# A four-block graph network on one core: two whole-state VectorE operations cut into tiles, and broadcast weight and bias rows read from PSUM

## The chip, the cores and the metric

The kernel runs on one core of one Trainium2 chip. The metric is the device time of one execution in microseconds (us); below 0.2% (about 9 us) a measurement of this kernel cannot tell a difference from no change.

## The reference, cut to what matters

A graph of 3125 nodes with 128 features and 53125 edges goes through four residual blocks. Each gathers a row per edge, scales it and sums it into the node that the edge points to. The second block does so five times (DEPTH = 5), with a layer norm that has a gain and a bias after each.

```python
h = relu(layernorm(x)); x = x + segment_sum(edge_weight * h[src], dst) @ W0.T + b0
h = relu(layernorm(x)); y = h
for i in range(5):
    Wf  = (ssp(rbf @ fw1[i] + fb1[i]) @ fw2[i] + fb2[i]) * C      # one filter row per edge
    agg = segment_sum((y @ lin1_w[i])[src] * Wf, dst) / degree
    y   = y + ssp(agg) @ lin2_w[i] + lin2_b[i]
    y   = (y - mean(y)) * rsqrt(var(y) + 1e-5) * ln_g[i] + ln_b[i]
x = x + y
...  # two more blocks of the same kind: one gated by tanh, one that only counts
```

## The kernel before, in words

Nodes are kept as `x`, `x2`, `y` [128 partitions, TILES = 25 tiles, 128 features], 3200 numbers in a partition; `u` is another name of `x`. The trace leaves numbers out of names, so `x2` is `x` there. Edges are worked in GROUPS = 52 groups of 1024. For each group GpSimd (POOL) issues eight indirect DMAs of 128 rows each (line 598, a "gather" below) into one of RING = 10 slots of `rows`. It may start a slot again once VectorE (DVE) has written the next indices into it (`stage`, line 1138).

The 52 groups are walked eight times: `first_edges` for the first block, `conv_edges` for each of the five layers (four in a device loop, `Fori(0, DEPTH - 1)`, and the last behind it), `gated_edges` and `count_edges`. A walk's gathers read the table that the walk before has written, so POOL starts a walk when the last rows of that table are stored.

In a layer, per group: TensorE (PE) makes hidden units and filters, ScalarE (ACT) and VectorE the softplus (`softplus_rest`, line 1335), VectorE adds the filter bias out of PSUM (`take_filters`, line 1342) and multiplies it by the gathered rows (`messages`, line 1348, which waits for the gathers of its group), and PE sums the messages into `sum_ps`, the first 80 columns of a bank of `pD`. The node work of finished blocks is put between the groups by hand (`conv_due`).

Each engine runs its own instructions in program order. `own(...)` makes VectorE wait for its own instruction before the next. Between two layers VectorE brings the state `y` up to date for the layer that begins (lines 1538 to 1541), before its first `softplus_rest`. Before the first layer it scales `y` and adds the bias (1518, 1519), and reads the node degrees, which PE writes into columns 0 to 24 of the same bank of `pD` (1522). Line 1513 adds the first block's bias row to `x`, and line 1543 the last layer's bias row to `x2`.

Of the kernel before, what the change touches and what calls it, by code (L numbers as in the profile page):

```python
# [21 lines left out]
ALU = mybir.AluOpType  # L22
# [3 lines left out]
P = 128  # L26
N_NODES = 3125
N_EDGES = 53125
D = 128
DEPTH = 5  # L30
# [16 lines left out]
TILES = -(-N_NODES // P)  # L47
# [22 lines left out]
def build(nc, a, out):  # L70
    ctx = ExitStack()
    with ctx:
        def sb(name, shape, dt=F32):
            return ctx.enter_context(nc.sbuf_tensor(name, shape, dt))

        def pb(name):
            return ctx.enter_context(nc.psum_tensor(name, [P, 2 * 512], F32))
# [54 lines left out]
        x = sb("x", [P, TILES, D])  # L132
        x2 = sb("x2", [P, TILES, D])
        u = x
        y = sb("y", [P, TILES, D])
# [6 lines left out]
        w0, w3, b0 = (node_log[:, n * D:(n + 1) * D] for n in range(3))  # L142
# [8 lines left out]
        mv = sb("mv", [P, TILES, 2])  # L151
        neg_mean = sb("neg_mean", [P, TILES])
        var = sb("var", [P, TILES])
        rstd = sb("rstd", [P, TILES])
# [16 lines left out]
        lb2 = sb("lb2", [P, DEPTH, D])  # L171
        ln_g = sb("ln_g", [P, DEPTH, D])
        ln_b = sb("ln_b", [P, DEPTH, D])
# [11 lines left out]
        pA, pB, pC, pD = pb("pA"), pb("pB"), pb("pC"), pb("pD")  # L185
# [2 lines left out]
        sum_ps = pD[:, 0:WIN]  # L188
        node_ps_all = pD[:, 512:1024]
        node_ps = node_ps_all[:, 0:2 * P]  # L190
        deg_sum_ps = pC[:, 0:WIN]

        dst_rows_loaded = sem("dst_rows_loaded")
# [78 lines left out]
        def over_tiles(row, n):  # L272
            return row.unsqueeze(1).broadcast_to([P, n, D])
# [226 lines left out]
        with nc.Block() as block:  # L500
# [553 lines left out]
            def _(dve):  # L1054
                n_pass = dve.value_load(passes_i[0:1, 0:1], min_val=1, max_val=MAX_PASSES)

                def own(ins):
                    ins.then_inc(dve_own, 1)
                    dve.wait_ge(dve_own, 1)
                    dve.sem_inc(dve_own, -1)  # L1060
# [114 lines left out]
                def improve_root(root, arg):  # L1175
                    dve.wait_ge(guess_full, 1)
                    dve.sem_inc(guess_full, -1)
                    tmp = newton[:, 0:root.shape[1]]
                    own(dve.scalar_tensor_tensor(tmp, root, -0.5, root, ALU.mult, ALU.mult))
                    own(dve.tensor_tensor(tmp, tmp, arg, ALU.mult))  # L1180
                    own(dve.scalar_tensor_tensor(root, tmp, 1.5, root, ALU.add, ALU.mult))
# [39 lines left out]
                def first_edges():  # L1221

                    def build(g):
                        match(onehot[:, g % 2, :, :], g).then_inc(onehot_full, 1)

                    with dve.Fori(0, n_pass):
                        build(0)
                        build(1)
                        for g in range(GROUPS + 1):
                            for b in done(g - 1):  # L1230
                                first_state(b)
                                node_deviation(b)
                                first_rows(b)
                            if g < GROUPS:
                                add_sums(g, degrees=True, rows_read=True)
                                if g + 2 < GROUPS:
                                    build(g + 2)
                            for b in done(g):
                                dve.sem_inc(agg_full, 1)
                        next_pass()  # L1240
                    last_sum()
# [170 lines left out]
                def begin_conv(l):  # L1412
                    dve.tensor_copy(fw1_l[:, :], fw1[:, l, :])
                    dve.tensor_copy(nfb1_l[:, :], nfb1[:, bass.ds(l, 1)]).then_inc(filter_ready, 1)
                    own(dve.tensor_copy(fb1_l[:, :], fb1[:, bass.ds(l, 1)]))
                    dve.sem_inc(bias_ready, 1)
                    start_sums()
# [81 lines left out]
                        next_pass()  # L1499
                    last_sum()  # L1500

                def over_nodes(tile):
                    return tile[:, :].unsqueeze(2).broadcast_to([P, TILES, D])


                dve.wait_ge(degs_set, 1)
# [3 lines left out]
                own(dve.tensor_tensor(dst0_g, dst0_g, base0[:, :].unsqueeze(2).broadcast_to([P, GROUPS, CH]), ALU.subtract))  # L1510
                start_windows()
                prepare_weights()
                dve.tensor_tensor(x[:, :, :], x[:, :, :], over_tiles(b0[:, :], TILES), ALU.add)
                first_edges()
                dve.sem_inc(deg_full, 1)
                begin_conv(0)

                own(dve.tensor_tensor(y[:, :, :], y[:, :, :], over_nodes(rstd), ALU.mult))
                own(dve.tensor_tensor(y[:, :, :], y[:, :, :], over_tiles(lb2[:, 0, :], TILES), ALU.add))
                dve.wait_ge(deg_ps, 1)  # L1520
                dve.sem_inc(deg_ps, -1)
                own(dve.tensor_scalar(deg_col[:, :], pD[:, 0:TILES], 1.0, None, ALU.max))
                dve.sem_inc(var_full, 1)
                improve_root(dcol[:, :], deg_col[:, :])

                own(dve.tensor_scalar(deg[:, :], deg[:, :], 1.0, None, ALU.max))
# [8 lines left out]
                with dve.Fori(0, DEPTH - 1) as l:  # L1535
                    conv_edges(l, last=False)
                    begin_conv(l + 1)
                    own(dve.tensor_tensor(y[:, :, :], u[:, :, :], mv[:, :, 0:1].broadcast_to([P, TILES, D]), ALU.subtract))
                    own(dve.tensor_tensor(y[:, :, :], y[:, :, :], over_nodes(rstd), ALU.mult))
                    own(dve.tensor_tensor(y[:, :, :], y[:, :, :], over_tiles(ln_g[:, l, :], TILES), ALU.mult))  # L1540
                    own(dve.tensor_tensor(y[:, :, :], y[:, :, :], over_tiles(lb2[:, l + 1, :], TILES), ALU.add))
                own(dve.memset(score[:, N_NODES:NPAD + WIN], 0.0))
                own(dve.tensor_tensor(x2[:, :, :], x2[:, :, :], over_tiles(ln_b[:, DEPTH - 1, :], TILES), ALU.add))
                conv_edges(DEPTH - 1, last=True)
                dve.sem_inc(dots_full, 1)
                start_sums()
# [26 lines left out]
```

## Time and profile before

| | |
|---|---|
| three runs | 4440.54, 4443.06 (median) and 4443.99 us |
| the profiled execution | 4444.43 us, of which the trace spans 4442.6 us |
| busy share of the span | POOL 73%, PE 56%, DVE 51%, ACT 48% |
| mean granted TensorE clock | 0.64 of full speed |

The 1.83 us that the profiled execution's time has over its span lie outside the trace. Busy shares are means over eight walks and their seams; the rows below look at the seams.

### The profile page before, as it was taken

What the parts mean: (1) busy time and instruction counts of PE and PEld (TensorE: products, weight loads), DVE (VectorE), ACT (ScalarE), POOL (GpSimd) and SP (SyncE); (2) the same over time, 40 slices, a digit from 0 to 9 for tenths busy, and PEclk for the clock granted to TensorE, in tenths of its full rate; (3) what the DMA queues carried; (4) which work ended last, traced back from release to release, by engine and by line L of the source; (5) the groups of instructions that cost most, each with busy time, mean ns of one, the idle gap of its engine ahead of it and who ended that gap; (6) DMA issues with size and microseconds to landing.
All of it is one profiled execution on the core that took longest, in us unless ns stands there. A gap on an engine that the chain in (4) does not pass through costs nothing. (4 is left out here: it accounts for less than half of the span.)

```text
span 4442.6 us, 56169 instructions
## 1 busy us (share of the span) xinstructions
PE 2495.7 (56%) x13164; PEld 2233.2 (50%) x13164; DVE 2255.9 (51%) x7419; ACT 2152.1 (48%) x5584; POOL 3251.0 (73%) x3339
## 2 busy tenths in 40 slices
PE   2554456666566665667656676567763333334334
PEld 2544456565455654656546566466663333333333
DVE  3322256666666666666666666677763333322221
ACT  2444456655566655665555665556653545510000
POOL 5777767777677776777767777677774777767776
PEclk8555567777677776777767777666665555555555
DMA  6333222222222222222222222222221222212221
GB/s 131 99 99 99 78 61 69 68 71 58 62 70 69 70 58 64 67 71 68 58 64 67 71 68 58 62 67 68 68 57 39 58 57 58 57 49 56 55 56 53
DMA packets 193643, 297.41 MB, mean 67 GB/s; under 512 B 81669, under 2 KB 116194, under 8 KB 193302
## 3 DMA queue, kind: packets, MB, share of 16 engines
q0 software_dynamic: 106496, 219.17, 19.2%
q10 hardware_dynamic: 33974, 57.75, 4.6%
q1 hardware_dynamic: 52832, 16.73, 1.6%
q8 instruction: 118, 1.93, 0.2%
q14 instruction: 223, 1.83, 0.1%
HBM read 272.15 MB, written 21.27 MB: 66 GB/s over the span
## 5 line engine op out<-in xcount | busy, mean ns | idle before, releaser
L598 POOL DMA_INDIRECT rows<-table,staged_src x3328 | 3244.4, 975 | 1175.8 <-issue 890.8
L770 PE MATMUL pD<-scatter,msg 128*128 128x80 f32 x4160 | 755.5, 357 | 682.1 <-PEq L768 673.9
L770 PEld LDWEIGHTS pD<-scatter,msg 128*128 128x128 f32 x4160 | 713.1, 266 | 757.7 <-issue 757.6
L691 PE MATMUL pD<-scatter,rows 128*128 128x80 f32 x2496 | 572.0, 423 | 665.2 <-PEq L683 360.5
L762 PE MATMUL pC<-fw,hidden 128*128 (+1 forms) x4160 | 819.5, 375 | 184.6 <-PEq L760 183.7
L691 PEld LDWEIGHTS pD<-scatter,rows 128*128 128x128 f32 x2496 | 544.4, 330 | 690.5 <-issue 690.5
L762 PEld LDWEIGHTS pC<-fw,hidden 128*128 128x128 f32 x4160 | 770.9, 284 | 216.0 <-issue 215.2
L908 ACT ACTIVATE scatter<-onehot,c_e 128x80 f32<-128x80 bf16 x2080 | 549.4, 346 | 669.1 <-ACTq L906 669.0
L1348 DVE TENSOR_TENSOR msg<-msg,rows 128x512 f32<-128x512 f32 x520 | 336.7, 688 | 592.9 <-DVEq L1142 588.1
L1131 DVE TENSOR_SCALAR onehot<-win,dst_rel 128x80 bf16<-128x80 f32 x2912 | 557.1, 285 | 31.4 <-DVEq L1060 31.1
L1138 DVE COPY staged_src<-src_i 128x8 int32<-128x8 int32 x416 | 76.0, 183 | 752.2 <-DVEq L1150 752.2
L942 ACT ACTIVATE hidden<-hidden 128x512 f32<-128x512 f32 x520 | 327.6, 630 | 63.6 <-ACTq L833 3.6
L941 ACT ACTIVATE hidden<-hidden 128x512 f32<-128x512 f32 x520 | 327.5, 630 | 62.9 <-ACTq L833 1.6
L1342 DVE TENSOR_TENSOR msg<-pC,fb 128x512 f32<-128x512 f32 x520 | 333.9, 681 | 8.2 <-DVEq L1341 8.1
L940 ACT ACTIVATE hidden<-pA,fb_l 128x512 f32<-128x512 f32 x260 | 176.2, 678 | 241.9 <-ACTq L950 241.9
L908 ACT ACTIVATE scatter<-onehot,w_e 128x80 f32<-128x80 bf16 x416 | 110.3, 347 | 276.1 <-ACTq L906 276.1
L1335 DVE SCALAR_TENSOR_TENSOR hidden<-pA,nfb_l,hidden 128x512 f32<-128x512 f32 x260 | 192.8, 741 | 59.5 <-DVEq L1334 59.4
L1335 DVE SCALAR_TENSOR_TENSOR hidden<-pB,nfb_l,hidden 128x512 f32<-128x512 f32 x260 | 193.3, 744 | 56.9 <-DVEq L1334 56.0
L1024 ACT ACTIVATE gate<-score,rows 128x80 f32 x416 | 110.6, 348 | 208.1 <-ACTq L1021 200.3
L752 PE MATMUL pA<-basis,fw_l 32*128 32x512 f32 x520 | 168.4, 723 | 36.6 <-PEq L749 36.6
L940 ACT ACTIVATE hidden<-pB,fb_l 128x512 f32<-128x512 f32 x260 | 174.0, 669 | 0.1
L752 PE MATMUL pB<-basis,fw_l 32*128 32x512 f32 x520 | 168.3, 723 | 0.0
(195 smaller groups left out, 1681.3 us busy)
## 6 DMA issues: line engine op xcount, KB each, us to landing
rows<-table,staged_src POOLq DMA_INDIRECT x3328
basis<-basis_d ACTq DMA_DIRECT2D x130, 256.0 KB, 2.8
table<-node_rows SPq DMA_DIRECT2D x66, 128.0 KB
msg<-in_edge_weight_dram ACTq DMA_DIRECT2D x54, 128.0 KB, 3.5
basis_d<-basis ACTq DMA_DIRECT2D x26, 256.0 KB, 3.7
hidden<-in_edge_weight_dram ACTq DMA_DIRECT2D x48, 128.0 KB, 3.3
table<-node_rows SPq DMA_DIRECT2D x11, 132.0 KB
out_dram<-node_rows SPq DMA_DIRECT2D x11, 128.0 KB
```

The lines of the kernel that those rows point to most:

```text
L598: pool.indirect_dma_start(out=rows[:, s, j, 0:width], out_offset=None, in_=tab[:, :], in_offset=bass.IndirectOffsetOnAxis(ap=staged_src[:, ...
L691: mm = pe.matmul(sum_ps, rows[:, g % RING, j, 0:D], scatter[:, g % 2, j, :], start=(j == 0), stop=(j == CH - 1))
L752: pe.matmul(hid_ps[n], fw1_l[at, :], basis[at, t % BASIS_RING, :], start=True, stop=True)\
L762: mm = pe.matmul(filt_ps[h][:, c * D:(c + 1) * D], hidden[:, strip(g, h), c * P:(c + 1) * P], fw2[:, l, :], start=True, stop=True)
L770: mm = pe.matmul(sum_ps, msg_of(g, h)[:, c * D:(c + 1) * D], scatter[:, g % 2, HALF * h + c, :], start=(h == 0 and c == 0), stop=(h == 1 a ...
L908: ins = act.activation(scatter[:, g % 2, j, :], onehot[:, g % 2, j, :], ACT.Copy, scale=weights[:, g * CH + j:g * CH + j + 1])
L940: own(act.activation(dst, arg, ACT.Abs, **bias))
L942: act.activation(dst, dst, ACT.Ln, bias=1.0).then_inc(full, 1)
L1131: ins = dve.tensor_scalar(dst[:, j, :], win[:, :], dst_rel[:, g * CH + j:g * CH + j + 1], None, ALU.is_equal)
L1335: dve.scalar_tensor_tensor(hidden[:, n, :], hid_ps[n], nfb1_l[:, 0:1], hidden[:, n, :], ALU.max, ALU.add).then_inc(ssp_full, 1)
L1342: dve.tensor_tensor(msg_of(g, h).rearrange("p (c d) -> p c d", d=D), filt_ps[h].rearrange("p (c d) -> p c d", d=D), over_tiles(fb2[:, l, : ...
L1348: dve.tensor_tensor(part, part, rows[:, g % RING, h * HALF:(h + 1) * HALF, 0:D], ALU.mult)\
```

## The change

Three things. The operations on the whole state that took a mean or a deviation per node from a broadcast tensor become one instruction per tile (25 of them), in which the mean and the deviation are scalars per partition; in the loop subtraction and multiplication become one instruction. Each broadcast row (gain, bias) is first copied from SBUF into a free part of the bank of `pD` (columns 128 to 511; `in_bank`), and the operation on the whole state reads it there. Before the first layer the bias is added behind the reading of the degrees instead of ahead of it.

```diff
+        spread_ps = pD[:, P:4 * P].rearrange("p (n d) -> p n d", d=D)
...
-                def over_nodes(tile):
-                    return tile[:, :].unsqueeze(2).broadcast_to([P, TILES, D])
+                def in_bank(n, row):
+                    own(dve.tensor_copy(spread_ps[:, n, :], row))
+                    return over_tiles(spread_ps[:, n, :], TILES)
+
+                def centred(state):
+                    for t in range(TILES):
+                        ins = dve.tensor_scalar(y[:, t, :], state[:, t, :], mv[:, t, 0:1], rstd[:, t:t + 1], ALU.subtract, ALU.mult)
+                    own(ins)
...
-                dve.tensor_tensor(x[:, :, :], x[:, :, :], over_tiles(b0[:, :], TILES), ALU.add)
+                dve.tensor_tensor(x[:, :, :], x[:, :, :], in_bank(0, b0[:, :]), ALU.add)
...
-                own(dve.tensor_tensor(y[:, :, :], y[:, :, :], over_nodes(rstd), ALU.mult))
-                own(dve.tensor_tensor(y[:, :, :], y[:, :, :], over_tiles(lb2[:, 0, :], TILES), ALU.add))
+                for t in range(TILES):
+                    ins = dve.tensor_scalar(y[:, t, :], y[:, t, :], rstd[:, t:t + 1], None, ALU.mult)
+                own(ins)
                 dve.wait_ge(deg_ps, 1)
                 dve.sem_inc(deg_ps, -1)
                 own(dve.tensor_scalar(deg_col[:, :], pD[:, 0:TILES], 1.0, None, ALU.max))
                 dve.sem_inc(var_full, 1)
+                own(dve.tensor_tensor(y[:, :, :], y[:, :, :], in_bank(1, lb2[:, 0, :]), ALU.add))
                 improve_root(dcol[:, :], deg_col[:, :])
...
-                    own(dve.tensor_tensor(y[:, :, :], u[:, :, :], mv[:, :, 0:1].broadcast_to([P, TILES, D]), ALU.subtract))
-                    own(dve.tensor_tensor(y[:, :, :], y[:, :, :], over_nodes(rstd), ALU.mult))
-                    own(dve.tensor_tensor(y[:, :, :], y[:, :, :], over_tiles(ln_g[:, l, :], TILES), ALU.mult))
-                    own(dve.tensor_tensor(y[:, :, :], y[:, :, :], over_tiles(lb2[:, l + 1, :], TILES), ALU.add))
+                    gain, bias = in_bank(0, ln_g[:, l, :]), in_bank(1, lb2[:, l + 1, :])
+                    centred(u)
+                    own(dve.tensor_tensor(y[:, :, :], y[:, :, :], gain, ALU.mult))
+                    own(dve.tensor_tensor(y[:, :, :], y[:, :, :], bias, ALU.add))
...
-                own(dve.tensor_tensor(x2[:, :, :], x2[:, :, :], over_tiles(ln_b[:, DEPTH - 1, :], TILES), ALU.add))
+                own(dve.tensor_tensor(x2[:, :, :], x2[:, :, :], in_bank(2, ln_b[:, DEPTH - 1, :]), ALU.add))
```

On VectorE, at the end of the loop body and behind the loop, the kernel before has these rows (line, operation, output and inputs, size, count; ISA and REGISTER_ALU rows set up addresses):

```order
L1538 TENSOR_TENSOR y<-x,mv 128x3200
L1539 TENSOR_TENSOR y<-y,rstd 128x3200
L1540 ISA
L1540 TENSOR_TENSOR y<-y,ln_g 128x3200
L1541 REGISTER_ALU
L1541 TENSOR_TENSOR y<-y,lb 128x3200
L1535 REGISTER_ALU
L1535 COMPARE_AND_BRANCH
L1542 MEMSET score 128x155
L1543 TENSOR_TENSOR x<-x,ln_b 128x3200
```

At the same place on VectorE the changed kernel has:

```order
L1504 ISA
L1504 COPY pD<-ln_g 128x128
L1504 REGISTER_ALU
L1504 COPY pD<-lb 128x128
L1509 TENSOR_SCALAR y<-x,mv,rstd 128x128 x25
L1549 TENSOR_TENSOR y<-y,pD 128x3200
L1550 TENSOR_TENSOR y<-y,pD 128x3200
L1544 REGISTER_ALU
L1544 COMPARE_AND_BRANCH
L1551 MEMSET score 128x155
L1504 COPY pD<-ln_b 128x128
L1552 TENSOR_TENSOR x<-x,pD 128x3200
```

Two of the four long operations have become 25 short ones, and the others, with the one behind the loop, take their row from `pD` after a copy each.

On VectorE ahead of the first layer, from the state's scaling to the first operation on `deg`, the kernel before has:

```order
L1518 TENSOR_TENSOR y<-y,rstd 128x3200
L1519 TENSOR_TENSOR y<-y,lb 128x3200
L1522 TENSOR_SCALAR deg_col<-pD 128x25
L1179 SCALAR_TENSOR_TENSOR newton<-dcol 128x25
L1180 TENSOR_TENSOR newton<-newton,deg_col 128x25
L1181 SCALAR_TENSOR_TENSOR dcol<-newton,dcol 128x25
L1526 TENSOR_SCALAR deg<-deg 128x3280
```

There the changed kernel has:

```order
L1526 TENSOR_SCALAR y<-y,rstd 128x128 x25
L1530 TENSOR_SCALAR deg_col<-pD 128x25
L1504 COPY pD<-lb 128x128
L1532 TENSOR_TENSOR y<-y,pD 128x3200
L1180 SCALAR_TENSOR_TENSOR newton<-dcol 128x25
L1181 TENSOR_TENSOR newton<-newton,deg_col 128x25
L1182 SCALAR_TENSOR_TENSOR dcol<-newton,dcol 128x25
L1535 TENSOR_SCALAR deg<-deg 128x3280
```

The long bias operation has moved from ahead of the degrees to behind them.

## Rows read from the trace of the kernel before

**Rows 1.** The page's first line, and line 598: duration in ns min/median/max.

```profile
span 4442.6 us, 56169 instructions
...
L598 POOL DMA_INDIRECT rows<-table,staged_src x3328: 940/944/4147, 35.1 to 4432.9; - x196
```

**Rows 2.** POOL's waits: us in total, times, longest us.

```profile
POOL rows L598 <- POOLq L596: 285.0, 405, 39.3
```

**Rows 3.** Timeline, second layer's start: start us, us, instruction [idle before <-releaser].

```profile
1131.37 4.01 POOL L598 DMA_INDIRECT rows<-table,staged_src  x1 [17.00 <-POOLq L596]
...
1134.72 3.49 DVE L1539 TENSOR_TENSOR y<-y,rstd 128x3200 f32<-128x3200 f32 x1
...
1135.69 3.34 POOL L598 DMA_INDIRECT rows<-table,staged_src  x1 [0.31 <-issue]
...
1156.84 1.29 DVE L1348 TENSOR_TENSOR msg<-msg,rows 128x512 f32<-128x512 f32 x2 [0.35 <-DVEq L1142]
```

**Rows 4.** Line 598 by stretch: us, POOL busy (gathers), PEclk, DMA share, GB/s.

```profile
80.80:84.20 3.40, 3.33 (x1) 0.50 0.08 22
575.10:583.10 8.00, 7.48 (x2) 0.50 0.03 8
1131.30:1146.60 15.30, 14.19 (x4) 0.50 0.34 99
2790.20:2809.70 19.50, 18.10 (x5) 0.50 0.27 81
606.80:739.50 132.70, 101.15 (x104) 0.72 0.25 67
1243.00:1343.90 100.90, 76.71 (x80) 0.79 0.26 70
```

**Rows 5.** Timeline at 71 us: VectorE reads PSUM while a gather is made.

```profile
71.75 0.81 DVE L1091 TENSOR_TENSOR lb<-lb,pB 128x640 f32<-128x640 f32 x1
71.82 0.94 POOL L598 DMA_INDIRECT rows<-table,staged_src  x1 [0.30 <-issue]
```

**Rows 6.** Timeline: VectorE operations with scalars, and the gather beside each.

```profile
586.78 1.87 DVE L1526 TENSOR_SCALAR deg<-deg 128x3280 f32<-128x3280 f32 x1
587.00 2.46 POOL L598 DMA_INDIRECT rows<-table,staged_src  x1 [0.30 <-issue]
...
2893.72 0.60 DVE L1388 TENSOR_SCALAR x<-x,mv,rstd 128x128 f32<-128x128 f32 x2 [0.15 <-DVEq L1060]
2893.90 0.99 POOL L598 DMA_INDIRECT rows<-table,staged_src  x1 [0.30 <-issue]
...
4101.40 1.65 DVE L1131 TENSOR_SCALAR scatter<-win,dst_rel 128x80 f32<-128x80 f32 x8 [0.24 <-DVEq L1060]
4102.07 0.94 POOL L598 DMA_INDIRECT rows<-table,staged_src  x1 [0.30 <-issue]
```

**Rows 7.** VectorE's groups by line and shape: busy us, mean ns | idle before.

```profile
L1388 DVE TENSOR_SCALAR x<-x,mv,rstd 128x128 f32<-128x128 f32 x25 | 7.6, 344 | 1.8 <-DVEq L1060 1.8
L1096 DVE TENSOR_SCALAR score<-lin,ln_gT 128x128 f32<-128x128 f32 x4 | 0.9, 283 | 0.1
```

**Rows 8.** Timeline, first layer: last gather of groups 0 and 14, and their messages.

```profile
591.02 0.94 POOL L598 DMA_INDIRECT rows<-table,staged_src  x1 [0.30 <-issue]
...
610.07 1.33 DVE L1348 TENSOR_TENSOR msg<-msg,rows 128x512 f32<-128x512 f32 x2 [0.35 <-DVEq L1142]
...
738.49 0.95 POOL L598 DMA_INDIRECT rows<-table,staged_src  x1 [0.30 <-issue]
...
741.77 1.29 DVE L1348 TENSOR_TENSOR msg<-msg,rows 128x512 f32<-128x512 f32 x2 [0.26 <-DVEq L1142]
```

**Rows 9.** VectorE's timeline ahead of the first layer, from the degrees on.

```profile
584.59 0.18 DVE L1522 TENSOR_SCALAR deg_col<-pD 128x25 f32<-128x25 f32 x1 [2.46 <-DVEq L1521]
585.76 0.21 DVE L1179 SCALAR_TENSOR_TENSOR newton<-dcol 128x25 f32<-128x25 f32 x1 [0.98 <-DVEq L1177]
...
594.92 3.49 DVE L1532 SCALAR_TENSOR_TENSOR x<-deg,score 128x3200 f32<-128x3200 f32 x1 [6.27 <-DVEq L1529]
```

## Prediction, before the changed kernel was run

> **What bounds the kernel now.** I read the page first, then POOL's waits, then the timeline at the seams between two walks. The 3328 gathers have a median of 0.944 us [rows 1] and 0.30 us from one to the next [rows 5], a period of 1.25 us, so undisturbed they alone take 3328 × 1.25 = 4150 of the 4442.6 us span. Does POOL wait inside a walk? Line 596 is its wait for a slot. Those 405 waits sum to 285.0 us, the longest 39.3 [rows 2]; at the usual 0.30 each they would be 122, and the other 163 are what the starts of the eight walks take: 17.00 at the seam of 1131 us [rows 3], 39.3 at one, and six more of that order. So inside a walk POOL issues without pause: it is the bound of every walk, though busy only 73%, and what lengthens a gather lengthens the kernel, unless the other engines are further behind.
>
> Now the seam at 1131 us, where the timeline shows what lengthens them. The gather issued at 1135.69 takes 3.34 us instead of 0.94; it ends at 1139.03, 0.82 after VectorE's operation of 1134.72 (3.49 us) has ended at 1138.21 [rows 3]. The undisturbed gather has those 0.82 us behind its first 0.12. So the reader sees a gather that gets stuck about 0.12 us in and goes on when the long VectorE operation ends. All four long operations of a seam do so: four gathers take 14.19 us [rows 4].
>
> **What the change takes away.** The stretches beside the seven places that are edited hold 1 gather in 3.33 us (the first block's bias), 2 in 7.48 (ahead of the first layer), 4 in 14.19 (this row stands for three seams of the loop that read alike) and 5 in 18.10 (last seam with the `x2` bias) [rows 4]. Together 3.33 + 7.48 + 3 × 14.19 + 18.10 = 71.5 us for 20 gathers; undisturbed these take 20 × 0.944 = 18.9. At stake: **52.6 us**, 1.2%.
>
> Whether it is freed depends on what the new instructions do to gathers.
>
> *Long operations with one input in PSUM.* The only ones of this kind before are shorter. At 71.75 one of 640 columns runs until 72.56; the gather of 71.82 would get stuck at 71.94, in the middle, and takes 0.94 [rows 5]. Cost to gathers: 0, from this row; from above, what the two-input form costs, 2.6 us an operation. I take 0, since the row has the same kind of operands. Here a rule speaks against the change. The Trainium skill (SBUF — State Buffer, § Who interferes with whom) states that a VectorE instruction with two SBUF inputs contends only with GpSimd work that reads SBUF, and infers that making descriptors needs only the write side; by that the long additions would not be what holds the gathers, and the sum would be 0. It disagrees with rows 3, where the gather's end follows the addition's end.
>
> *25 short instructions.* A long scalar operation does hold a gather: 1.87 us of it make one 2.46 [rows 6]. Short ones in a string do not: a whole gather of 0.94 us passes inside eight of them at 4102.07, and beside the pair with two scalars, the new form, the gather takes 0.99, 0.05 over the median [rows 6]. A string meets about five gathers at a seam, four ahead of the first layer: 24 × 0.05 = **1.1 us given back**. The bounds are 0 and a string that holds a gather to its end (a rival below).
>
> *VectorE's own time.* The pair takes 0.60 us, one of the pair 0.344 [rows 6, 7], so the next starts 0.26 later: 24 × 0.26 + 0.34 = 6.6 us for `centred` in place of two times 3.49. With one scalar, 4 take 0.9 at a mean of 0.283 [rows 7]: 0.2 apart, 5.1 us in place of 3.49. A copy into PSUM has no row; the nearest are 0.28 (128 columns, SBUF) and 0.81 (640 columns, out of PSUM), and I take 0.3 with 0.15 of waiting. A seam was 4 × 3.49 + 0.6 of waits = 14.6 and becomes 0.9 + 6.6 + 7.0 + 0.3 = 14.8 us. Reading PSUM does not slow it: 0.81 for 640 columns is 1.27 ns a column with its fixed part, 3.49 for 3200 is 1.09. VectorE thus starts the layer as late as now, and is no faster.
>
> *Ahead of the first layer.* The bias now stands behind the degrees: 0.45 + 3.49 + 0.15, less the 0.98 us of waiting that it covers [rows 9], is 3.1 us more before ACT gets `deg`; behind it wait the operation at 594.92 and all of VectorE's first edge work.
>
> **What is late next.** The gathers come earlier, VectorE does not, so the edge work lags more. Now, in the second layer, group 0's last gather ends at 1151.5 (1143.08 + 3.40, then 0.30 and three periods and 0.94) and its messages start at 1156.84 [rows 3]: a lag of 5.4. It becomes 5.4 + 10.4 = 15.8. In the first layer the lag is 610.07 − 591.96 = 18.1, and 741.77 − 739.44 = 2.3 fourteen groups later [rows 8]. Of these 15.8 some 4.7 were gathers held by two more long operations, which stay; 11.1 were made up, **0.8 us a group**. So 15.8 is gone after 18 groups, the first layer's 18.1 + 5.6 + 3.1 = 26.8 after about 26, of 52. POOL may be ten groups ahead, 100 us, so it never waits for a slot. At a walk's end the messages again follow the gathers, and what POOL saved arrives whole.
>
> One thing is given back on the way. While lagging, messages (two-input operations too) fall on gathers at random: 101.15 us for 104 gathers, 0.029 over the median; in step it is 76.71 for 80, 0.015 [rows 4]. The difference is 0.11 us a group. Groups that lag additionally: 13 in each of three layers, 11 in the first, 17 in the last, 67 in all: **7.6 us**.
>
> **Sum.** −52.6 + 1.1 + 7.6 = −43.9. The profiled execution's 4444.43 becomes 4400.5; on the median, 4443.06 − 43.9 = **4399 us**, 1.0% less.
>
> **The rivals.** (a) *The string holds a gather to its end.* The Trainium skill (same page and section) has scalar operations in the modes that hold the shared port for a whole instruction; back to back, 25 may leave no gap. Then one gather a seam waits some 5.9 us, four times, and one 5.0 ahead of the first layer: 28.6 in place of 1.1, with 4 less given back through lag: 4423 us. For it: the long scalar operation of rows 6. Against it: both strings there.
>
> (b) *The lag isn't made up in the last layer*, whose node work per block is greater. Its 13.4 us (18.10 − 5 × 0.944) are then lost: 4412. It decides below 0.3 us a group; the 0.8 is from the first layer, and I have no such stretch of the last.
>
> (c) *Long operations from PSUM hold gathers all the same*: two a seam at 2.5, with 2.4, 2.4 and 2.9 for the three single ones, 27.5 us stay: 4423. Against it: rows 5.
>
> (d) *Nothing changes*, because something else at a walk's start lengthens gathers: 4443. Against it: the gather at 591.02 in the same start takes 0.94 [rows 8].
>
> (e) *Slower: a gather under way holds each short instruction.* The string then takes one gather period per instruction, 25 × 1.25 = 31 us, 24.7 more a seam and 26 ahead of the first layer. The lag starts at 40.5 in the loop's layers; it costs time from where it cannot be made up in 52 groups beyond the 10.4 saved, below 0.58 us a group. At 0.5 it leaves 4.1 in each of three layers, 16 in the first and 2 in the last; with the 2.4 saved in the first walk, +28: 4471. Beside it stands the rule (same section) that the order of issue decides who is blocked. Against it: the string of eight took 1.65 us with a whole gather inside [rows 6].
>
> **How the numbers follow.** The forecast 0.70, with a range of its own of 4390 (all 52.6 freed) to 4407 (lag costs twice as much); (a) 0.08, (b) 0.10, (c) 0.04, (d) 0.03, (e) 0.05. From 4388 to 4424 us the range holds the forecast, (a), (b) and (c); the low end adds 2 us for messages that happen to meet fewer gathers. Faster by over 0.2% 0.92, within 0.2% (what a measurement can tell from no change) 0.03, slower 0.05.
>
> **What would show it.** In the profile after, the four gathers at each seam should take about 1.0 us each, so POOL's next ones start some 10 us earlier after the walk's first; the seams themselves should stay near 17 us; the 25 short instructions should last 6.6 us, the operations reading `pD` 3.49; in the layers VectorE should not wait for gathers (line 1142 of before) for the first 18 groups or so, then wait as now; each walk's last gather should end earlier against its first by 10 us in the loop's layers, 5.6 in the first, 13 in the last, less 1 to 2. Wrong would be: a gather of 6 us beside the string (a), of 3.4 beside an operation from `pD` (c), messages that still trail by more than 2 us at the end of a layer (b), a string of 20 us or more (e).

## The result, and the profile after

| | before | changed |
|---|---|---|
| median | 4442.17 us (4440.54 to 4443.99) | 4400.27 us (4393.84 to 4401.15) |
| runs | 4 | 4 |
| ratio | | 0.9902 [0.9885, 0.992] |
| profiled execution | 4444.43 us | 4393.84 us |

The changed kernel is 1.0% faster, 41.9 us by the medians; 4399 was forecast. Its profiled execution is 6 to 7 us shorter than its other three runs; the last experiments return to that.

The page's first line and its group of the gathers, which are line 599 now (busy us, mean ns | idle before); [rows 1] had a span of 4442.6. The same group in the kernel before stands last:

```profile
span 4392.0 us, 56303 instructions
...
L599 POOL DMA_INDIRECT rows<-table,staged_src x3328 | 3193.7, 960 | 1175.7 <-issue 892.3
...
L598 POOL DMA_INDIRECT rows<-table,staged_src x3328 | 3244.4, 975 | 1175.8 <-issue 890.8
```

POOL's waits (us in total, times, longest), against 285.0, 405 and 39.3 in [rows 2]:

```profile
POOL rows L599 <- POOLq L597: 283.4, 400, 39.6
```

POOL waits as it did. What became shorter is the gathers themselves: 3328 at a mean of 960 ns in place of 975; an undisturbed one takes 944, the median.

The second layer's start in the timeline of the changed kernel, for [rows 3]:

```profile
1121.25 0.94 POOL L599 DMA_INDIRECT rows<-table,staged_src  x1 [17.03 <-POOLq L597]
1121.42 0.29 DVE L1504 COPY pD<-ln_g 128x128 f32 x1 [0.25 <-DVEq L1061]
...
1122.38 6.53 DVE L1509 TENSOR_SCALAR y<-x,mv,rstd 128x128 f32<-128x128 f32 x25 [0.15 <-DVEq L1061]
...
1126.24 1.00 POOL L599 DMA_INDIRECT rows<-table,staged_src  x1 [0.30 <-issue]
1127.54 0.97 POOL L599 DMA_INDIRECT rows<-table,staged_src  x1 [0.30 <-issue]
...
1129.06 3.49 DVE L1549 TENSOR_TENSOR y<-y,pD 128x3200 f32<-128x3200 f32 x1
...
1130.06 0.94 POOL L599 DMA_INDIRECT rows<-table,staged_src  x1 [0.30 <-issue]
...
1142.05 0.75 DVE L1336 SCALAR_TENSOR_TENSOR hidden<-pA,nfb_l,hidden 128x512 f32<-128x512 f32 x1 [5.87 <-issue]
...
1149.55 1.29 DVE L1349 TENSOR_TENSOR msg<-msg,rows 128x512 f32<-128x512 f32 x2 [0.35 <-DVEq L1143]
...
1357.39 1.29 DVE L1349 TENSOR_TENSOR msg<-msg,rows 128x512 f32<-128x512 f32 x2 [0.39 <-DVEq L1143]
```

The gather of 1130.06 lies wholly inside a multiplication of 3.49 us that reads its row from `pD`, and takes 0.94; before, its counterparts took 3.34 and more. The worst beside these 25 short instructions takes 1.00.

The gathers by stretch (us, POOL busy with them and their number, PEclk, DMA share, GB/s): the four edited places, for the first four of [rows 4], then the five layers from first gather to last:

```profile
80.60:84.20 3.60, 2.83 (x3) 0.50 0.20 55
572.00:580.00 8.00, 6.01 (x7) 0.50 0.16 43
1121.20:1137.00 15.80, 12.09 (x13) 0.50 0.44 133
2754.50:2774.50 20.00, 15.17 (x16) 0.50 0.39 115
572.00:3287.00 2715.00, 2014.37 (x2080) 0.70 0.24 67
```

In the same kind of stretch the seam after the first layer had held 4 gathers of 3.55 us; it now makes 13 of 0.93 (one that the stretch cuts counts in part). The five layers of the kernel before:

```profile
575.00:3337.00 2762.00, 2061.40 (x2080) 0.71 0.24 66
```

2061.40 − 2014.37 = 47.0 us of the 50.6 by which the span shrank are gather time in the layers. By walk, from the start of its first gather to the end of its last, as the timeline has them (us):

| walk | first block | layer 1 | 2 | 3 | 4 | 5 | gated | count |
|---|---|---|---|---|---|---|---|---|
| before | 522.58 | 539.21 | 536.13 | 535.74 | 536.04 | 546.64 | 520.69 | 519.12 |
| changed | 519.78 | 532.06 | 527.40 | 527.55 | 527.32 | 532.38 | 519.91 | 519.01 |
| shorter by | 2.8 | 7.2 | 8.7 | 8.2 | 8.7 | 14.3 | 0.8 | 0.1 |

The seams between the walks stay: 17.03, 17.01, 17.01 and 17.01 at the starts of the second to the fifth layer, and 39.62 behind the last layer (39.31 before). The first layer became shorter by 7.2 us, though only 5.6 were at stake there; in three other profiles of the changed kernel it lasts 534.0 to 535.5, 3.8 to 5.2 us less than before.

### The profile page after: what moved, and what is told of

The parts are those of the page before. It is cut to its first block and busy times, and to the rows that moved or that the text cites. A ratio compares the mean times of both kernels' runs of the same rounds, so it can differ in the third digit from the quotient of the medians.

```text
span 4392.0 us, 56303 instructions
## 1 busy us (share of the span) xinstructions
PE 2484.7 (57%) x13164; PEld 2218.7 (51%) x13164; DVE 2259.8 (51%) x7546; ACT 2152.2 (49%) x5584; POOL 3200.3 (73%) x3339
## 3 DMA queue, kind: packets, MB, share of 16 engines
q0 software_dynamic: 106496, 219.17, 18.5%
## 5 line engine op out<-in xcount | busy, mean ns | idle before, releaser
L599 POOL DMA_INDIRECT rows<-table,staged_src x3328 | 3193.7, 960 | 1175.7 <-issue 892.3
L763 PEld LDWEIGHTS pC<-fw,hidden 128*128 128x128 f32 x4160 | 758.1, 279 | 271.3 <-issue 271.0
L1157 DVE TENSOR_TENSOR agg<-agg,pD 128x80 f32 x416 | 97.6, 235 | 200.9 <-DVEq L1151 114.5
```

The lines of the kernel that those rows point to most:

```text
L599: pool.indirect_dma_start(out=rows[:, s, j, 0:width], out_offset=None, in_=tab[:, :], in_offset=bass.IndirectOffsetOnAxis(ap=staged_src[:, ...
L763: mm = pe.matmul(filt_ps[h][:, c * D:(c + 1) * D], hidden[:, strip(g, h), c * P:(c + 1) * P], fw2[:, l, :], start=True, stop=True)
```

## The experiments

Two theories of what holds a gather stood against each other at first: long operations with two SBUF inputs hold it and an input in PSUM sets it free; or else it is their length, or something else at a walk's start. Later runs ask whether the lag of VectorE costs anything, and where the rest of the gather time is.

**Rows in PSUM alone.** Mean and deviation are broadcast operations on the whole state again, ahead of the first layer too; the rows still come from `pD`. Cut to the loop:

```diff
...
-                    centred(u)
+                    own(dve.tensor_tensor(y[:, :, :], u[:, :, :], mv[:, :, 0:1].broadcast_to([P, TILES, D]), ALU.subtract))
+                    own(dve.tensor_tensor(y[:, :, :], y[:, :, :], over_nodes(rstd), ALU.mult))
...
```

> The changed kernel with its mean and deviation again as two long operations with a broadcast tensor; only the gain and bias rows are read from PSUM. Theory (a long VectorE operation holds a gather only when both its inputs lie in SBUF): the two long operations with two SBUF inputs hold one gather each as before, (4.01 + 3.34 - 1.89) = 5.5 us a seam, four times, and about 3.2 us ahead of the first layer; the gathers beside the operations that read PSUM take 0.94. Time: 4400 + 25, less some 4 us of lag = about 4421 us. Rival 1 (the length of the operation is what holds a gather, wherever its inputs lie): all four gathers of a seam take 3.3 us and more, about 4440 us. Rival 2 (only the PSUM rows matter): about 4400 us.

4423.07 us (4420.22 to 4427.05; before 4446.19), ratio 0.9951 [0.9935, 0.9968]. Its timeline at the second layer's start has both kinds of operation:

```profile
1126.02 3.49 DVE L1549 TENSOR_TENSOR y<-x,mv 128x3200 f32<-128x3200 f32 x1
...
1126.51 3.82 POOL L599 DMA_INDIRECT rows<-table,staged_src  x1 [0.30 <-issue]
...
1129.66 3.49 DVE L1550 TENSOR_TENSOR y<-y,rstd 128x3200 f32<-128x3200 f32 x1
...
1130.63 3.34 POOL L599 DMA_INDIRECT rows<-table,staged_src  x1 [0.30 <-issue]
...
1133.30 3.49 DVE L1551 TENSOR_TENSOR y<-y,pD 128x3200 f32<-128x3200 f32 x1
...
1134.28 0.94 POOL L599 DMA_INDIRECT rows<-table,staged_src  x1 [0.30 <-issue]
```

Same engine, same shape, same 3.49 us: the two with both inputs in SBUF hold a gather until 0.82 us after their own end (1129.51 to 1130.33), the one that reads `pD` holds none. That settles it for long operations with two inputs: neither length nor place, but the second SBUF input. It holds in the other places too: each of the nine such operations that this run keeps in the layers holds one gather (3.33 to 4.16 us), as each of the 19 does in the kernel before, and of the gathers that start beside one of the 44 operations on `pD` in four profiles of the changed kernel none takes over 0.95. A long operation with a scalar, and one SBUF input, holds a gather all the same [rows 6].

**Scalars by tile alone.** The 25 short instructions stay; the rows are read from SBUF.

```diff
                 def in_bank(n, row):
-                    own(dve.tensor_copy(spread_ps[:, n, :], row))
-                    return over_tiles(spread_ps[:, n, :], TILES)
+                    return over_tiles(row, TILES)
```

> The changed kernel with gain and bias rows read from SBUF again; only the mean and deviation stay as 25 short instructions. Theory (both parts count, each for the gathers beside it): the gathers beside the short string take about 0.95 us, those beside the two long operations 3.4, so 27.5 us come back of the 52.6: 4400 + 27.5, less some 4 us of lag = about 4423 us. Rival (one part did it all): about 4400 or about 4440 us.

4429.26 us (4426.97 to 4432.64), ratio 0.9963 [0.9951, 0.9976], 6 us less gain than my theory said. Its timeline at the same place:

```profile
1130.13 6.50 DVE L1508 TENSOR_SCALAR y<-x,mv,rstd 128x128 f32<-128x128 f32 x25 [0.15 <-DVEq L1061]
...
1136.88 3.49 DVE L1548 TENSOR_TENSOR y<-y,ln_g 128x3200 f32<-128x3200 f32 x1 [0.25 <-DVEq L1061]
...
1137.79 3.40 POOL L599 DMA_INDIRECT rows<-table,staged_src  x1 [0.30 <-issue]
```

The halves act apart: 23.1 us for the rows, 16.9 for the scalars, 40.0 together, against 46.5 for both, measured beside them (below). The 95% intervals of the ratios are some 6 to 7 us wide to either side, so the missing 6 are not clear of the noise. The profiles point at a place for them. In the layers, gathers beside the long operations took 50.2 us above 0.944 each before; with the rows in PSUM alone 24.2 of it stay, with the scalars alone 25.9, so each half frees what it edits. The other gathers of the layers took 47.7 us above it before (49.7 in a second profile); this is 52.9 and 55.7 with one half, and 50.9 to 58.2 in four profiles with both. So one half gives back about as much as both do, and the 4 us that my theories took off for a smaller lag were not seen.

**Short operations with two SBUF inputs.** Gain and bias, and the single bias rows, as 25 additions or products of one tile each, from SBUF; eleven strings in all.

```diff
+                def by_tile(state, row, op):
+                    for t in range(TILES):
+                        ins = dve.tensor_tensor(state[:, t, :], state[:, t, :], row, op)
+                    return ins
...
-                    own(dve.tensor_tensor(y[:, :, :], y[:, :, :], gain, ALU.mult))
+                    own(by_tile(y, ln_g[:, l, :], ALU.mult))
```

> The changed kernel with gain and bias applied tile by tile, 25 instructions of 128 columns each with both inputs in SBUF, no copy into PSUM. Theory (a gather that finds the port taken goes on when the VectorE instruction under way ends, so that short instructions cost it little wherever their inputs lie): gathers beside these strings take 0.94 to 1.1 us; VectorE needs about 5 us a string in place of 3.5, which lies off the path: 4400 to 4404 us. Rival (back to back, two-input instructions leave no gap, and the gather is held to the end of the string): one gather of about 5 us beside each string, 10 strings, 4400 + 10 x 4 = about 4440 us; then reading from PSUM is what the change lives on.

4431.14 us (4425.88 to 4435.82), ratio 0.9967 [0.9956, 0.9978]: the theory that cutting is enough fell. It is no faster than the run before, which reads the same rows from SBUF in long operations (4429.26). Its timeline at two layers' starts, the first of them an exception:

```profile
1688.58 5.31 DVE L1505 TENSOR_TENSOR y<-y,ln_g 128x128 f32<-128x128 f32 x25 [0.25 <-DVEq L1061]
...
1689.83 0.94 POOL L599 DMA_INDIRECT rows<-table,staged_src  x1 [0.30 <-issue]
...
2787.05 5.14 DVE L1505 TENSOR_TENSOR y<-y,ln_g 128x128 f32<-128x128 f32 x25 [0.25 <-DVEq L1061]
...
2788.21 4.79 POOL L599 DMA_INDIRECT rows<-table,staged_src  x1 [0.30 <-issue]
...
2792.41 5.14 DVE L1505 TENSOR_TENSOR y<-y,lb 128x128 f32<-128x128 f32 x25 [0.22 <-DVEq L1061]
...
2793.31 1.01 POOL L599 DMA_INDIRECT rows<-table,staged_src  x1 [0.30 <-issue]
...
2794.63 3.74 POOL L599 DMA_INDIRECT rows<-table,staged_src  x1 [0.30 <-issue]
```

The gather of 2788.21 ends at 2793.00, 0.81 after the string ends at 2792.19: back to back, 25 short instructions can hold a gather as one long one does. Not every gather: that of 2793.31 passes inside the next string in 1.01, and the one behind it is held. Of the eleven strings eight hold one gather each (3.53 to 4.79 us), six of them after letting one pass, and three hold none, among them that of 1688.58.

The three took 5.30, 5.31 and 5.45 us instead of 5.14, but a string of 5.34 held a gather for 4.64, so a little more length is not the reason. The single instructions of the trace show where the length comes from: in the three, all gathers but one start within 0.011 us of an instruction's start, and that instruction takes 0.31 to 0.33 us in place of 0.28. But five of the eight gathers that were held started as close to an instruction. What decides whether a gather passes stays open.

**The changed kernel again**, beside the three:

> The changed kernel once more, for the spread of its times and a second profile. Theory (what is given back through lagging messages differs from run to run): times between 4393 and 4402 us, and the gathers' time over the median, summed over the first to last layer, differs between the two profiles by about what the spans differ by. Rival (the spread comes from elsewhere, the start or the seams): the same sum over the layers, and another length of a seam or of the start.

4399.7 us (4393.55 to 4402.36), ratio 0.9898 [0.9881, 0.9914].

**More work of VectorE at the seam.** `centred(u)` is done twice, then four times; the result is the same, only time is added.

```diff
-                    centred(u)
+                    for _ in range(2):
+                        centred(u)
```

> The changed kernel with the 25 short instructions of each of the four seams in the loop done twice (same result, 6.5 us more of VectorE at each seam). Theory (VectorE's time at a seam lies off the path, the lag is made up within the layer): the lag of group 0 grows from 18 to 25 us, the gathers stay as they are, the time grows by 1 to 4 us, to about 4402 us. Rival (VectorE's time at a seam is on the path): +26 us, about 4426 us.

4403.64 us (4400.27 to 4404.08; before 4446.69), ratio 0.9903 [0.9887, 0.992]. The second layer's first messages lag by 25.2 us, as expected. 26 us more of VectorE's work in four seams cost 3 to 4, which is within the noise, and not the rival's 26.

> The same with three strings more, 19.7 us of VectorE at each of four seams. The lag of group 0 grows from 18 to 38 us; at the 0.7 us a group by which the second layer of the changed kernel makes it up, 51 groups take 36 us. Theory (off the path as long as the layer can make it up): 0 to 3 us left over at a layer's end, with more messages on gathers 4 to 14 us more, 4404 to 4414 us. Rival (on the path): +79 us, about 4479 us.

4420.02 us (4409.61 to 4421.11), ratio 0.9941 [0.9924, 0.9957]: 78 us more cost about 20, some 6 more than my upper figure, and nowhere near the 4479 of work that lies on the path. In its profiled execution (4409.61) the second layer's first messages lag by 38.0 us and the seams read 16.9 to 18.3, so the lag is made up; that execution has 2027.57 us of gathers in the layers, 13.2 more than the changed kernel. Why the other three runs were 9.6 to 11.5 us longer still, no profile shows.

**The degrees in pieces.** Three long operations ahead of the first layer, which the change left, cut by tile; the second of them is shown:

```diff
...
-                own(dve.scalar_tensor_tensor(tmp, deg[:, 0:NPAD], -1.0, guess, ALU.mult, ALU.mult))
+                for t in range(TILES):
+                    part = slice(t * P, (t + 1) * P)
+                    ins = dve.scalar_tensor_tensor(tmp[:, part], deg[:, part], -1.0, guess[:, part], ALU.mult, ALU.mult)
+                own(ins)
...
```

> The changed kernel with the three operations on deg ahead of the first layer (held gathers: 1.7, 2.3 and 2.4 us) cut into 26, 25 and 25 pieces of 128 columns: the first has one input in SBUF and constants, the other two have two inputs in SBUF. Theory after the run with short two-input strings (what counts is the second input in SBUF, and a string of such instructions without gaps holds a gather to its end): beside the first string gathers take 0.95 us, beside each of the two others one takes 3.5 to 5 us; time within 4 us of the changed kernel. Rival (short instructions let a gather through): all gathers there 0.94 to 1.1 us, 6 us less, about 4394 us.

4400.83 us (4398.7 to 4403.13), ratio 0.9895 [0.9879, 0.9912], no gain, as the theory had it. The rival's 6 us would hardly stand out of the intervals; its timeline decides:

```profile
587.29 4.08 DVE L1537 TENSOR_SCALAR deg<-deg 128x128 f32<-128x128 f32 x26
587.35 0.98 POOL L599 DMA_INDIRECT rows<-table,staged_src  x1 [0.30 <-POOLq L597]
...
597.64 5.14 DVE L1546 SCALAR_TENSOR_TENSOR x<-deg,score 128x128 f32<-128x128 f32 x25 [6.28 <-DVEq L1541]
...
599.86 3.73 POOL L599 DMA_INDIRECT rows<-table,staged_src  x1 [0.30 <-issue]
```

Short operations with one SBUF input let gathers pass, though the whole one of 1.87 us does not [rows 6]; those with two hold one gather a string, as in the third experiment.

**Messages that read PSUM.** The largest remainder is beside `messages`. Here the filter bias is added in place in PSUM and the product reads PSUM and `rows`; the filters' bank comes free only behind the product. Cut to the product:

```diff
...
                 def messages(g, h):
                     part = msg_of(g, h).rearrange("p (c d) -> p c d", d=D)
-                    dve.tensor_tensor(part, part, rows[:, g % RING, h * HALF:(h + 1) * HALF, 0:D], ALU.mult)\
-                       .then_inc(msg_full, 1)
+                    dve.tensor_tensor(part, filt_ps[h].rearrange("p (c d) -> p c d", d=D),
+                                      rows[:, g % RING, h * HALF:(h + 1) * HALF, 0:D], ALU.mult)\
+                       .then_inc(filt_free, 1)
...
```

> The changed kernel with the filter bias added in place in PSUM, so that the product with the gathered rows (the operation that holds most of the remaining gather time, 32 us in the profile) has one input in PSUM and one in SBUF. PE can then make the next group's filters only after the product, so up to 3.7 us of PE work a group goes behind the gathers. Theory (gathers set the pace; PE has 2 to 3 us of waiting a group): gathers in the layers take 0.95 us, 30 us less, about 4370 us. Rival (the filters' way over product, filters, sums becomes the bound, over 10 us a group): gathers undisturbed but POOL waiting for slots or messages trailing to the layer's end, 4400 to 4600 us.

4970.17 us (4964.49 to 4970.63), ratio 1.1177 [1.1159, 1.1196]; my theory of a gain was wrong, and the loss was greater than the rival's. Its gathers within a layer (windows, as above):

```profile
1228.30:1742.00 513.70, 386.05 (x408) 0.73 0.25 68
```

and its waits (us in total, times, longest):

```profile
DVE pC L1344 <- DVEq L1342: 649.4, 516, 2.0
...
POOL rows L598 <- POOLq L596: 882.1, 376, 153.2
```

The gathers are free: 386.05 / 408 = 0.946 us each, beside products of 512 columns all along. But VectorE now waits 1.26 us for each half of the filters, since PE may not write them before the product of the group before is done; the group takes longer than POOL's eight gathers, and POOL waits 882 us instead of 283. Most of it waits between the walks, 121 us at each of four seams in place of 17 and 153 behind the last layer in place of 40: the ten slots hide the growing lag until the layer ends, where the messages trail the gathers by over 100 us. The bound has moved to the chain from product to filters.

**Three more profiles**, of the changed kernel twice and of the kernel before once:

> The changed kernel, one profile more. The two profiles so far are of executions at 4393.6 and 4393.8 us, while the timed ones cluster at 4400. Theory (what differs from execution to execution is how many gathers the lagging messages hold): over several profiles the span rises with the time that gathers are held beside the product of messages and rows (32.4 and 35.5 us so far), near one for one. Rival (the difference lies at the start or the seams): that time stays within 3 us while spans differ by 6, and the seams differ.

> The same kernel and the same question as the look before it: a span with its time of gathers held by messages, 4392 with some 33 us, or 4398 to 4400 with some 40 us, if the theory holds.

> The kernel before, one profile more. Theory: its messages lag for 15 groups in the first layer only and 5 in the others, so its time of gathers held by messages stays near the 33.5 us of the first profile, and its executions differ less than those of the changed kernel: 4440 to 4449 us with 33 to 37 us held. Rival (held gathers differ as much in the kernel before): 40 us and more.

4401.56, 4401.57 and 4446.57 us, one execution each. The gathers of the five layers in the first of them:

```profile
572.20:3293.70 2721.50, 2020.44 (x2080) 0.70 0.25 67
```

in the second:

```profile
572.00:3294.30 2722.30, 2021.65 (x2080) 0.70 0.25 66
```

in the third, of the kernel before:

```profile
575.10:3339.20 2764.10, 2063.26 (x2080) 0.71 0.24 65
```

and in the earlier profile of the changed kernel (4393.55 us):

```profile
571.20:3288.10 2716.90, 2016.12 (x2080) 0.71 0.25 67
```

With the profile after, four executions of one program have 2014.4, 2016.1, 2020.4 and 2021.7 us of gathers in the layers, and spans of 4392.0, 4391.7, 4399.8 and 4399.8. Added up over all gathers that overlap an operation of `messages` (line 1349), what each takes above 0.944 is 39.8, 41.5, 45.2 and 45.5 us in the same order; the figures in the expectations come from another count. So the messages hold the gathers longer in one execution than in another. Some 6 us of it in the layers go with 8 of span, not one for one, but it is most of why the profiled execution after was shorter than the median. The kernel before has 35.3 and 37.1 us by this count, and 2061.4 and 2063.3 us of gathers: the rival's 40 and more was not seen.

## Why the prediction was right

**The bound.** It holds: POOL's waits hardly changed, its gathers became shorter, and the walks with them.

**52.6 us at stake.** Freed as forecast, except for a few hundredths at some gathers beside a string. Long operations that read `pD` cost gathers 0, the value taken from [rows 5]; the two operations in the first experiment show it side by side. One argument was better than its evidence: the row of [rows 5] is of 640 columns and a fifth as long.

Behind (d) stood the Trainium skill (SBUF — State Buffer, § Who interferes with whom): two SBUF inputs contend with GpSimd's reads, and descriptors, it infers, need only the write side. Here the trace disagrees with what is inferred, 3.34 and 3.82 us against 0.94 in one timeline, and the measurement decides. With the first half it need not disagree: the gather has `staged_src`, its row numbers in SBUF, as an input. No run shows which part of a gather is held.

**The 25 short instructions.** 6.53 us against 6.6, and ahead of the first layer 5.09 against 5.1. Beside the five strings gathers take 0.94 to 1.07, in all 0.4 to 0.7 us above the undisturbed in the four profiles, where the sum has 1.1: most pass at 0.94 to 0.95. The copy takes 0.29 against 0.3. By-form groups of the changed kernel (busy us, mean ns | idle before):

```profile
L1509 DVE TENSOR_SCALAR y<-x,mv,rstd 128x128 f32<-128x128 f32 x100 | 26.0, 362 | 0.6 <-DVEq L1061 0.3
L1549 DVE TENSOR_TENSOR y<-y,pD 128x3200 f32<-128x3200 f32 x4 | 13.9, 3488 | 0.6
```

Both strings of [rows 6] have one SBUF input. The theory of the third experiment took them as evidence for short instructions in general and fell; the change uses only those with one SBUF input.

**The lag.** Undersized by about 3 us, right in kind. In the second layer group 0's messages start at 1149.55, behind a last gather that ended at 1131.00: 18.5 us against 15.8. Group 22's start at 1357.39, 1.75 behind theirs (1355.64), so 16.8 us were made up in 22 groups, 0.76 a group against 0.8. Ahead of the first layer, in the timeline:

```profile
572.02 5.09 DVE L1526 TENSOR_SCALAR y<-y,rstd 128x128 f32<-128x128 f32 x25
...
581.03 0.94 POOL L599 DMA_INDIRECT rows<-table,staged_src  x1 [0.30 <-issue]
...
582.46 3.49 DVE L1532 TENSOR_TENSOR y<-y,pD 128x3200 f32<-128x3200 f32 x1
...
610.50 1.32 DVE L1349 TENSOR_TENSOR msg<-msg,rows 128x512 f32<-128x512 f32 x2 [0.35 <-DVEq L1143]
```

The lag there is 610.50 − 581.97 = 28.5, against 26.8. The seam of VectorE was 14.8 us as forecast; what was missed is its wait behind it. Before its first softplus operation in the second layer VectorE stands idle 5.87 us; before the change it was 3.34. The wait stands behind the branch back to the loop's head, and it goes with the program: at the three returns it is 5.4 to 5.9 us in all four profiles of the changed kernel, and 3.2 to 3.6 in both of the kernel before and in the first three experiments. These 2 to 2.5 us are most of what the sum lacked. What VectorE waits for there was not tried.

**7.6 us given back.** The term with the largest spread; by the prediction's own figures (0.11 × 67) it is 7.4, not 7.6. The gathers of the layers had 2061.40 − 2080 × 0.944 = 97.9 us above the undisturbed before, of which 50.2 were at the edited places (52.6 less the 2.4 of the first walk); 47.7 remained. After there are 50.9, 52.6, 56.9 and 58.2 in the four executions: 3.2, 4.9, 9.2 and 10.5 given back, where the sum has 1.1 + 7.6 = 8.7. In the two at 4401.6 us, close to the median, it is 9 to 10.5. Against the second profile of the kernel before each is about 2 us less. That the median came out 1 us from the forecast is therefore luck in part: this one term ranges over 7 us between executions. That messages hold more gathers when they lag is borne out by the run with three strings more: 52.8 us above the undisturbed beside messages (46.0 with one string more), against 39.8 to 45.5 in the changed kernel and 35.3 and 37.1 before.

**The rivals.** (a) fell by the gathers of 0.94 to 1.07 beside the strings; its mechanism is real for two inputs in SBUF. (c) fell by the gather of 1130.06, (d) by the time itself, (e) by strings of 5.09 and 6.5 us (its price had a slip: by the steps given the first layer leaves 21 us and not 16, so 4476). (b) fell at the last layer's end. The changed kernel's last gather of the layers and the last two messages:

```profile
3285.93 1.00 POOL L599 DMA_INDIRECT rows<-table,staged_src  x1 [0.30 <-issue]
...
3297.28 0.69 DVE L1349 TENSOR_TENSOR msg<-msg,rows 128x512 f32<-128x512 f32 x1 [0.26 <-DVEq L1143]
...
3301.86 0.69 DVE L1349 TENSOR_TENSOR msg<-msg,rows 128x512 f32<-128x512 f32 x1 [0.26 <-DVEq L1147]
```

The messages trail the last gather's end (3286.93) by 10.35 and 14.9 us; in the kernel before they trail by 10.1 and 14.6:

```profile
3336.00 0.94 POOL L598 DMA_INDIRECT rows<-table,staged_src  x1 [0.30 <-issue]
...
3347.00 0.69 DVE L1348 TENSOR_TENSOR msg<-msg,rows 128x512 f32<-128x512 f32 x1 [0.26 <-DVEq L1142]
...
3351.57 0.69 DVE L1348 TENSOR_TENSOR msg<-msg,rows 128x512 f32<-128x512 f32 x1 [0.26 <-DVEq L1146]
```

So the lag of 17 us with which the layer began is gone. My test for (b), messages within 2 us of the gathers, would have misled: node work stands between them in both kernels, and only the comparison tells.

## What to carry to other kernels

Where GpSimd issues indirect transfers without pause, look for VectorE operations with two SBUF inputs: each long one held one gather for the rest of its length here (some 2.6 us), and cutting it into short ones back to back did not help. Moving one input into PSUM, or making it a scalar per partition in short instructions, freed the transfers, though VectorE got no faster. A lag of the consumers cost little while they worked faster than the producer and the ring was deep (3 to 4 us for 26 us of added work, 20 for 78); but a consumer that must hand back its own input's bank can become the bound, as in the run of 4970 us.

## What the runs showed of the hardware that was not expected

- 25 back-to-back operations of 128 columns with two SBUF inputs held one gather to the end of the string in eight strings of eleven (4.79 us beside 5.14), most of them after another had passed, and none in three. What decides is open.
- An operation with one SBUF input holds a gather to its end when it is long (1.87 us of it make one 2.46, [rows 6]), and not as 26 short ones (0.98 at most). Why the short ones differ from those with two inputs, the runs don't say.
- One program's spans spread by 8 us, and the time that messages hold its gathers varies with them (39.8 to 45.5 us); what sets that in an execution stays open.
- Behind the branch back to a loop's head VectorE stood idle 3.2 to 3.6 us in the kernel before and 5.4 to 5.9 in the changed one, in every profile of each; why was not tried.
